# Indirect transfers spaced by other GpSimd work, and gate products moved from ScalarE to GpSimd, in a fused attention and mixture-of-experts kernel

## The reference

```
xn  = layernorm(x)
qkv = xn @ w_qkv.T ; scores = q @ k.T / sqrt(8) ; out = softmax(scores) @ v
attn = out @ w_proj.T + b_proj
h = xn @ W_in + b_in ; probs = softmax(h @ W_gate + b_gate)       # 8 experts
top 2 experts per row, their two weights scaled to sum 1 (the gates)
e-th expert: relu(h @ W1[e] + b1[e]) @ W2[e] + b2[e]              # 128 -> 512 -> 128
ffn = (sum over the two of gate * expert output) @ W_out + b_out
result = x + attn + ffn
```

## Time and profile before

| | |
|---|---|
| time, median of 3 runs | 299.69 us (294.74 to 300.15) |
| profiled execution: own time, span | 294.88 us, 293.1 us |
| PE, PEld busy | 238.7 us (81%), 207.7 us (71%) |
| DVE, ACT, POOL busy | 153.5 us, 126.3 us, 126.8 us |
| mean granted TensorE clock | 0.918 |
| L597 (low part, DVE) | 56 instructions, mean 718 ns |
| L342 and L365 (indirect DMAs, POOL) | 32 each, mean 995 and 990 ns |
| L334 (copy of a tile's weights, POOL) | 39, mean 1164 ns |
| chain that ended last | PE 66%, DVE 11%, "another core or an unknown queue" 10%, ACT 6% |

### The profile page before, as it was taken

One profiled execution on the slowest core, in us unless ns is written; L12 is line 12 of the kernel. 1 busy time (PEld: TensorE's weight loads), 2 busy tenths in 40 slices (PEclk: granted clock), 3 DMA queues, 4 the chain that ended last, 5 costly groups with the idle time before them and its releaser, 6 DMA issues.

```text
span 293.1 us, 4452 instructions
## 1 busy us (share of the span) xinstructions
PE 238.7 (81%) x1507; PEld 207.7 (71%) x1507; DVE 153.5 (52%) x345; ACT 126.3 (43%) x296; POOL 126.8 (43%) x147
## 2 busy tenths in 40 slices
PE   7897838469797778999999999997523199999995
PEld 6796726358675568999999999774313087788894
DVE  5746865335876344444444444677201036776453
ACT  1553300016462453444444444664110248687661
POOL 4049517741877303566665552377777100000000
PEclk9999786959999999999999999999755569999999
DMA  6799201110011210222222221021111000000001
GB/s 196 316 308 328 68 0 55 54 36 0 21 45 54 67 31 20 72 75 64 73 73 65 74 72 39 27 58 47 51 54 54 18 36 2 0 0 36 2 5 68
DMA packets 23046, 19.52 MB, mean 67 GB/s; under 512 B 3280, under 2 KB 19696, under 8 KB 22768
## 3 DMA queue, kind: packets, MB, share of 16 engines
q1 hardware_dynamic: 20000, 14.71, 16.6%
q0 software_dynamic: 2048, 4.20, 4.8%
q10 hardware_dynamic: 976, 0.33, 0.4%
HBM read 10.97 MB, written 8.26 MB: 66 GB/s over the span
## 4 chain that ended last, share of the span: by engine, by line
PE 66%; DVE 11%; another core or an unknown queue 10%; ACT 6%; issue 3%; DMA 2%; ACTq 1%
PE ps L1024 12%; PE ps L1010 12%; PE ps L837 5%; DVE part_max L587 5%; PE ps L780 5%; PE ps L778 4%; PE ps L779 4%; PE ps L911 4%; PE ps L907 4%; PE ps L908 3%; PE ps L786 3%; DVE pl L597 2%; ACT pf L437 2%; PE ps L899 2%
## 5 line engine op out<-in xcount | busy, mean ns | idle before, releaser
L597 DVE TENSOR_TENSOR pl<-pf,ph 128x512 fp32r<-128x512 f32 x56 | 40.2, 718 | 60.8 <-ACT pf L437 51.4
L334 POOL COPY wst<-wtab 128x1156 f32 x39 | 45.2, 1164 | 49.8 <-DVE y_sb L725 40.3
L436 ACT ACTIVATE ph<-ps 128x512 fp32r<-128x512 f32 x56 | 33.6, 600 | 65.6 <-PE ps L780 31.6
L437 ACT ACTIVATE pf<-ps 128x512 f32<-128x512 f32 x64 | 38.0, 594 | 23.7 <-PE ps L780 12.3
L587 DVE TENSOR_REDUCE part_max<-ps 128x1 f32<-128x1024 f32 x32 | 38.9, 1220 | 17.0 <-PE ps L837 9.5
L1024 PE MATMUL ps<-wst,mid 128*128 128x128 f32 x312 | 41.3, 275 | 0.9 <-DVE x_sb L615 0.9
L1010 PE MATMUL ps<-xgT,wst 128*128 128x128 f32 x312 | 41.3, 275 | 0.0
L837 PE MATMUL ps<-xnT_hi,q_hi 128*128 128x512 f32 x64 | 23.5, 453 | 20.7 <-DVE part_max L587 20.1
L342 POOL DMA_INDIRECT slots_in<-hl,slots x32 | 31.9, 995 | 18.6 <-DVE slots L664 9.3
L365 POOL DMA_INDIRECT wtab<-slots_out,slots x32 | 31.7, 990 | 17.7 <-issue 9.5
L717 DVE TENSOR_SCALAR mid<-ps,wst 128x128 f32<-128x128 f32 x78 | 23.7, 345 | 28.9 <-PE ps L1010 28.9
(11 more groups left out here) (145 smaller groups left out, 331.6 us busy)
## 6 DMA issues: line engine op xcount, KB each, us to landing
wtab<-in_L_ffn_W_dram SPq DMA_DIRECT2D x16, 256.0 KB, 6.0
xg<-slots_in SPq DMA_DIRECT2D x39, 64.0 KB, 1.9
slots_out<-y_sb SPq DMA_DIRECT2D x39, 64.0 KB, 1.5
slots_in<-wst SPq DMA_DIRECT2D x2, 1024.0 KB, 5.0
x_sb<-in_L_attn_x_dram SPq DMA_DIRECT2D x4, 256.0 KB, 5.1
out_dram<-x_sb SPq DMA_DIRECT2D x3, 256.0 KB, 2.4
wtab<-in_L_ffn_b_dram SPq DMA_DIRECT2D x1, 512.0 KB, 7.4
slots_in<-hl,slots POOLq DMA_INDIRECT x32
```

Source lines behind the costliest of these rows:

```text
L334: pool.tensor_copy(wst[:, t % 4, :], wtab[:, bass.ds(experts[t], 1), :].rearrange("p a n -> p (a n)")).then_inc(Z["staged"], 1)
L437: act.activation(pf[:, i % 3, :], ps[:, st_bank(i), :], ACT.Exp).then_inc(Z["pf_done"], 1)
L597: dve.tensor_tensor(pl[:, i % 3, :], pf[:, i % 3, :], raw(ph[:, i % 3, :]), ALU.subtract).then_inc(Z["lo_done"], 1)
```

## The change

GpSimd now adds the biases to only two tiles ahead of the scatters (`UNTIED = 2`). The other 14 additions stand one by one behind the scatters numbered 4 to 17, so that four scatters stand bare (`BARE = 4`). The copies of the weights of tiles 0 to 3, which stood together between scatters 15 and 16, now stand behind scatters 20, 23, 26 and 29, with the wait for the experts ahead of the first of them. Each group's `add_out` waits for the biases of its own tiles.

Behind the experts, `weigh` leaves ACT's list and goes to GpSimd's as a `tensor_scalar`: behind the two gathers of tile j stands the product of tile j-2, which waits for its two transfers. DVE's `combine` gets a wait for the transfers beside the one for the product. The steps at which `combine` stands are as before.

```diff
+    BARE, UNTIED = 4, 2
+    STAGE_AT = [20, 23, 26, 29]
...
-            for j in range(NT):
+            def bias(j):
                 pool.tensor_tensor(x_sb[:, j, :], x_sb[:, j, :], bsum[:, 0, :], ALU.add).then_inc(Z["x_biased"], 1)
+            for j in range(UNTIED):
+                bias(j)
...
-            for j in range(NT // 2):
-                scatter(j)
-            pool.wait_ge(Z["experts_ready"], 1)
-            pool.wait_ge(Z["tab_loaded"], 16 * (2 * NE + 1))
-            pool.wait_ge(Z["wT_copied"], 5)
-            load_experts(0, 8)
-            for t in range(4):
-                stage(t)
-            for j in range(NT // 2, NT):
-                scatter(j)
+            for n in range(TOPK * NT):
+                j, c = n // TOPK, n % TOPK
+                pool.indirect_dma_start(out=slots_in, out_offset=bass.IndirectOffsetOnAxis(ap=slots[:, c, j:j + 1], axis=0),
+                                        in_=hl[:, j, 0:D], in_offset=None).then_inc(Z["scattered"], 16)
+                if UNTIED + n - BARE in range(UNTIED, NT):
+                    bias(UNTIED + n - BARE)
+                if n in STAGE_AT:
+                    if n == STAGE_AT[0]:
+                        pool.wait_ge(Z["experts_ready"], 1)
+                        pool.wait_ge(Z["tab_loaded"], 16 * (2 * NE + 1))
+                        pool.wait_ge(Z["wT_copied"], 5)
+                        load_experts(0, 8)
+                    stage(STAGE_AT.index(n))
...
+            def weigh(j):
+                pool.wait_ge(s_z[j], 32)
+                pool.tensor_scalar(z[:, j, 0, :], z[:, j, 0, :], gate1[:, j:j + 1], None, ALU.mult).then_inc(Z["z_weighed"], 1)
+
+            pool.wait_ge(Z["gates_ready"], 1)
             for j in range(NT):
                 for c in range(TOPK):
                     pool.indirect_dma_start(out=z[:, j, c, :], out_offset=None, in_=slots_out,
                                             in_offset=bass.IndirectOffsetOnAxis(ap=slots[:, c, j:j + 1], axis=0)
                                             ).then_inc(s_z[j], 16)
+                if j >= 2:
+                    weigh(j - 2)
+            weigh(NT - 2)
+            weigh(NT - 1)
...
-            def weigh(j):
-                act.wait_ge(s_z[j], 32)
-                act.activation(z[:, j, 0, :], z[:, j, 0, :], ACT.Copy, scale=gate1[:, j:j + 1]).then_inc(Z["z_weighed"], 1)
-            act.wait_ge(Z["gates_ready"], 1)
...
-                    for j in weighed_at(s):
-                        weigh(j)
...
-                if g == 0:
-                    dve.wait_ge(Z["x_biased"], 1 + NT)
+                dve.wait_ge(Z["x_biased"], 1 + first + TILES[g])
...
             def combine(j):
+                dve.wait_ge(s_z[j], 32)
                 dve.wait_ge(Z["z_weighed"], j + 1)
```

## The result

The changed kernel takes 266.64 us (median of 4 runs, 266.23 to 267.97) against 297.46 us for the kernel before on the same chip (4 runs, 294.74 to 300.15): a ratio of 0.9043, with 0.8999 to 0.9087 as its interval. It is faster: by some 31 us between the medians, by some 28 by the ratio. The forecast was 266.0, with a range of 255 to 300. The profiled execution took 267.97 us itself and its span is 266.2.

What follows compares the result with a forecast made beforehand. Prediction: PE's finished work reaches ACT and DVE late while POOL issues indirect DMAs unpaused. Last combine 240.5 + experts' shift 2.0 + remainder 22.1 = 264.6 us span, + 1.8 = 266 us; range 255 to 300.

Steps and rivals of the forecast that it cites:

- The mechanism: Scatters and gathers: unpaused indirect DMAs make PE's finished work known late to ACT and DVE, up to 18.5 us; spacing cures it.
- Rival A: Scatters and gathers: events stay late as long as the stream lasts, whatever its spacing; 306 us, chance 0.15.
- Rival B: Gathers: spacing a little short, delay begins 30 to 35 us into the stream, 13 us lost; 279 us, 0.20 with C.
- Rival C: POOL: each change between transfers and arithmetic costs more than 0.3 us; 280 us, up to 298; 0.20 with B.
- The scatters: Ahead of the experts: 14 scatters with a bias at 1.95 us each, 27.3 in all; last scatter ends at 100.1, not 98.13.
- The registers: POOL between scatter 20 and the first weight copy: 1.0 us, as from 71.24 to 72.25 in the earlier trace.
- The experts: Expert stage behind the scatters: later by 2 us (2.0 - 1.0 + 1.0), between -3 and +5.
- The product on POOL: Behind each tile's two gathers: 0.43 us, bounds 0.29 and 0.59; a tile 3.2 us, combine(15) at 239.3 at the earliest.
- The steps: Beside and behind the gathers: first 15 steps at 1.71 us each, then 29.25 for 15 to 31; last combine at 240.5.
- DVE held by POOL's products: At the first combines: DVE waits a us or two; products were to set its pace at 3.2 us a tile.
- Contention: Biases and products beside DVE's low: taken as 0, with 7 us kept in the range, sum up to 273.
- The balance band: Indirect DMA stream: a spacing of 1.5 to 1.7 us would be in balance, estimated from fill and empty times.

Runs made afterwards that it cites:

- experiment 2: Changed kernel with its scatters kept, but the 32 gathers bare and the products back on ACT: 289.75 us, ratio 0.9804 to the kernel before.
- 3: Changed kernel with products back on ACT and a 640-column GpSimd memset behind every second gather: 264.66 us, ratio 0.8986 to the kernel before.
- 4: Changed kernel with products back on ACT and a 16-column memset behind each gather, still 1.25 to 1.26 us apart: 292.64 us, ratio 0.9922.
- 5 to 8: Changed kernel, products on ACT; memset of 256 or 128 columns per gather, 4 us pause per eight, or bare half-row gathers: 264.69 to 265.32 us, kernel before 263.05.
- 11: Changed kernel with all biases ahead of the scatters, two pauses in these, products on ACT, 640-column memset behind every second gather: 263.51 us, ratio 0.8861.
- 12: Changed kernel with products on ACT and a 256-column memset behind every gather, on a chip with late events: 263.58 us, ratio 0.8947 to the kernel before.
- experiment 10: Changed kernel with products on ACT, gathers in eights with 4 us of memsets behind each eight, on a third chip: median 271.12 us.

## Why the prediction was right, point by point

**The mechanism held.** The reading of the earlier trace rows, that what PE has finished is known late while POOL issues indirect DMAs without a pause, is borne out by runs that differ in the spacing and in little else: experiment 2 against 3, 25 us apart, and against 4, where POOL does more work but at the old spacing. As a late event can be put down to "issue", the pace of the steps is the safer sign: steps 9 to 15 take 15.24 to 15.29 us in all of 3, 5 to 8, 11 and 12, on chips with the effect and without, and 41 in the kernel before. What was taken from the trace alone (begin and end with the stream) turned out to be cause and effect.

**Rival A** (late whatever the spacing) asked for "remote" waits on a longer stream. The stream of gathers is longer (185.00 to 236.74, against 187.04 to 228.18) and there are none. The Trainium skill, page "SBUF — State Buffer", § Who interferes with whom, says that DMA never contends with a compute engine and that PE and ACT wait on no one. It says so of the ports of SBUF, and the conclusion drawn from it, that spacing could not help, went further and is refuted for these chips: experiments 2 and 3 show PE's work reaching ACT 16.7 us late or not, by the pace of DMAs issued elsewhere. Where on the way it is held up, and whether SBUF has a part in it, no run shows. **Rival B** (spacing a little short) did not come; its delay would have begun 43 us into the stream by its own proportion (13 us at an excess of a third), not 30 to 35. **Rival C** (dear changes of work) came out with the opposite sign.

**The size: two misses cancelled.** Predicted for the last `combine` was 240.5 + 2.0 = 242.5, measured 244.12; behind it 22.1 us in both. Inside:

- *The scatters.* 1.95 us each was too much: the surcharge of 0.25 over the plain 1.70, for the change between arithmetic and transfers, is not paid behind a bias. The scatter takes 0.97 to 0.99 and its gap shrinks to 0.17, so a scatter and a bias cost 1.62 to 1.65 in twelve cases of fourteen (2.00 and 2.43 in the other two), 24.2 in all where 27.3 was put. The price came from the one scatter behind a weight copy; there it holds, with 1.23 to 1.30 for the scatter behind each of the four copies, but a bias was no such neighbour. The 1.0 for the registers wasn't there either. The last scatter ended at 96.67, not at 100.1; inside the bounds.
- *The experts* began 2.8 us sooner than now (99.76 for 102.59) instead of some 1 later; PE had waited 6.20 us for them, not near 10. At step 0 that is -2.1, against the +2 of the sum: **4.1 us too pessimistic**.
- *The product on POOL* was priced 0.43 with an upper bound of 0.59; it takes 0.62 to 1.18, 0.77 at the median, and even the shortest is above the bound. The addition of the same shape was not a fair neighbour, and what the product takes beyond 0.62 comes from a contention (below). As a transfer behind it has a gap of 0.17, a tile is 3.35 us, not 3.2, and POOL's last product ended at 239.15, where the prediction had 239.3 plus the shift.
- *The steps* are where **the failed term** is. Steps 0 to 9 took 15.36 us (15.35 predicted) and 15 to 31 took 29.30 (29.25). But the six between, 9 to 15, which the trace of before shows only in their disturbed form, were put at 1.71 each, 10.3 in all. They took 16.43, with PE busy 12.97 (second window above). Four of them in a row hold a pair of maxima; PE waits on DVE's reading of these three times, ahead of two pairs and ahead of the transposes behind them, for 3.5 us in all. The last two hold the first transposes and projection of a block. With the products on ACT (experiment 12) they still take 15.24 (196.70 to 211.94), so 4.9 us were missed in the pace itself and 1.2 in the new wait. The steps ahead were the wrong measure: no row of before shows these six undisturbed, and what they hold besides the products of a step would have had to be counted.
- *DVE held by POOL's products:* three waits, 2.1 us in all, the longest 0.96 at 200.76. That is the "us or two" of the prediction; but the products didn't set DVE's pace at 3.2 us a tile, as it had said of what would show it, since the other thirteen `combine` show no such wait. Steps 0 to 31 take 61.1 us, against 59.9 in experiments 3 and 12, so it costs 1.2.
- *Contention.* `low` takes 764 ns at the mean, 718 before. Beside the gathers it is 715 ns (30 of them, 184 to 242 us), against 691 to 693 in experiments 3 and 12, which have no such product: 0.7 us in all, close to the 0 that was taken. Most of the rise is beside the weight copies that now stand between the scatters: nine `low` from 76.5 to 99 us take 1.05 at the mean, against 0.71 for the seven ahead of them, most of which run beside the biases. Two rows beside a copy, and the `low` beside the product at 196.62 (above):

```profile
76.88 1.89 DVE L609 TENSOR_TENSOR pl<-pf,ph 128x512 fp32r<-128x512 f32 x1 [0.67 <-ACT pf L456]
77.05 1.16 POOL L343 COPY wst<-wtab 128x1156 f32 x1
...
196.41 0.69 DVE L609 TENSOR_TENSOR pl<-pf,ph 128x512 fp32r<-128x512 f32 x1
```

Beside a copy it is `low` that gets longer: three take 1.08 to 2.35 us, and each ends 0.55 us behind its copy's end. The experts waited for the scatters then, so that it cost nothing. In the gathers `low` mostly starts first, and the product gets longer: the four products that meet no `low` take 0.62, and nine that start as a `low` does or while it runs take 0.76 to 1.18, longer by the rest of that `low` less 0.14 to 0.24. The remaining three fit less well: the two from 236.77 on, and the one at 223.30, which starts ahead of a `low` and holds up nothing. The Trainium skill (same page and section) says that one of the pair wholly blocks the other, and up to 7 us were kept for it; the trace agrees in the main, and in the gathers POOL paid for it, with some 3.0 us against the 0.7 of `low`.

**The balance band** of 1.5 to 1.7 us was too high: experiment 12 runs clean at 1.44 to 1.46, though its average of 1.55 lies in the band. It also falls as a model. A queue that fills by the difference between asked and given pace would, for 18.5 us of lateness after 32 transfers, need 0.58 us more for each than the 1.25 they have, so a balance near 1.8; 1.46 would not do. And with a balance at 1.46 or below, eights at 1.25 would be 1.7 us behind at most, and the pause of 4 us would clear that; an event was 3.8 us late all the same (experiment 10, another chip). So lateness isn't simply the sum of the excess; what it follows is open.

## What to carry to other kernels

Where PE, ACT and DVE wait on one another with "remote" as the releaser while GpSimd issues indirect DMAs back to back, put some 0.3 us of GpSimd work behind each transfer, or 0.65 behind every second, rather than 4 us behind eight; useful work if there is some, a memset if not, and check the gain on more than one chip, since on a chip without the effect the four kernels run there lost about 1%. When a disturbed stretch is to be priced undisturbed, count what its steps hold; the pace of the steady steps next to it is a lower bound. And read a spacer's cost by what it adds to the period of the stream: the first 0.13 us vanish in the gap that is there already. And where the work is to run beside a VectorE operation that reads two tiles from SBUF, expect one of the two to take longer (here a product 0.62 to 1.18 us, and `low` up to 2.35 beside a weight copy).

## What had not been expected of the hardware

**The effect depends on the chip.** The kernel before took 295.76 to 299.69 us at the median in every other comparison, and 263.05 on the chip of experiments 5 to 8, some 33 to 37 us less, with none of its 25 runs above 265.67. There all four kernels were slower than it by 0.8 to 1.1% (1.0078, 1.0109, 1.0085, 1.0085, each interval above one). The fourth has bare gathers, though of half the rows, and loses as much, so the loss can't be put down to the spacing of the gathers; what all four have in common are the scatters as changed. The kernel before was not profiled on that chip and the changed kernel not run; that the difference is the late events is inferred from the absence of any in the four traces taken there, among them bare gathers, 1.20 us apart, of half the rows. The forecast of 266 us holds on the chips that have the effect; on the other one the change would likely lose a per cent.

**Late events come in lumps, not in proportion.** Spaced by 1.44 us and more there are none (experiment 12), nor in pairs 1.25 us apart with 2 us behind each pair (experiment 3); in eights 1.25 us apart an event is 3.8 us late within the third eight and none within the first two (experiment 10, one trace), and ACT starts 18.5 us late once 32 are out without a pause. Which resource PE's events share with POOL's transfers no run here shows.
